# Full attention: who reads the turned row maxima out of PSUM, and who waits for whom over a score slot

## The reference

```python
scores = jnp.einsum('bhqd,bhkd->bhqk', q, k) / np.float32(np.sqrt(HD))
attn = jax.nn.softmax(scores, axis=-1)
out = jnp.einsum('bhqk,bhkd->bhqd', attn, v)
```

## Time and profile before

| | us |
|---|---|
| median of 3 runs | 4466.62 (4456.62 to 4467.39) |
| profiled execution, its own time | 4465.89 |
| its span, first to last instruction | 4464.1 |
| around the span | 1.79 |
| full attention, exponentials only | 279.2 to 1677.6 |
| first 31 groups' part of it | 278 to 1622 |

### The profile page before, as it was taken

The page is one execution under the profiler, slowest core; times in us unless marked ns, Lnnn a source line. Parts: engine busy times, 40 slices in busy tenths (PEclk is TensorE's granted clock), DMA queues, the critical chain, the costliest instruction groups (busy, mean ns, idle before and its releaser), DMA issues. The chain is left out here.

```text
span 4464.1 us, 79549 instructions
## 1 busy us (share of the span) xinstructions
PE 4130.9 (93%) x26918; PEld 2629.4 (59%) x26918; DVE 3555.6 (80%) x7972; ACT 2784.3 (62%) x6236; POOL 1568.3 (35%) x2441
## 2 busy tenths in 40 slices
PE   6679999999999986499999998999899999998998
PEld 3323333333333324377777776888777777777887
DVE  6589999999999957788888886656688888885665
ACT  3438888888888871167766665444567666663343
POOL 0000001000000003456655554454456555554555
PEclk9979999999999987799999999999999999998999
DMA  6833343233332306510000100221010010101321
GB/s 223 283 55 55 50 77 57 41 57 46 52 53 44 57 7 210 163 44 26 25 26 27 39 24 19 86 60 55 20 48 25 25 28 25 39 17 57 88 72 56
DMA packets 366416, 274.97 MB, mean 62 GB/s; under 512 B 98921, under 2 KB 333241, under 8 KB 366017
## 3 DMA queue, kind: packets, MB, share of 16 engines
q1 hardware_dynamic: 364608, 269.02, 24.7%
q10 hardware_dynamic: 1408, 0.93, 0.1%
HBM read 165.98 MB, written 102.81 MB: 60 GB/s over the span
## 5 line engine op out<-in xcount | busy, mean ns | idle before, releaser
L881 ACT ACTIVATE fa_P<-fa_pS 128x512 f32<-128x512 f32 x2048 | 1111.7, 595 | 324.9 <-PE fa_pS L805 276.1
L908 DVE TENSOR_REDUCE fa_mx<-fa_pR 128x2 f32<-128x1024 f32 x1024 | 1205.3, 1220 | 92.0 <-PE fa_pR L786 77.6
L1668 POOL TENSOR_TENSOR wa_pn<-wa_pr,wa_ri 128x512 f32<-128x512 f32 (+1 forms) x512 | 673.1, 1316 | 495.4 <-DVE wa_ri L1720 495.1
L1606 ACT ACTIVATE wa_pr<-wa_sm,wa_mn 128x256 f32<-128x256 f32 (+1 forms) x1024 | 496.7, 488 | 177.8 <-DVE wa_mn L1711 151.5
L822 PE MATMUL fa_pO<-fa_P,fa_V 128*32 128x512 f32 x4096 | 555.6, 615 | 0.0
L805 PE MATMUL fa_pS<-fa_Q,fa_K 50*128 50x512 f32 x2048 | 512.0, 497 | 41.9 <-ACT fa_P L881 11.2
L805 PEld LDWEIGHTS fa_pS<-fa_Q,fa_K 50*128 50x128 f32 x2048 | 192.6, 185 | 526.5 <-ACT fa_P L881 439.7
L786 PE MATMUL fa_pR<-fa_K,fa_Q 48*128 48x512 f32 x2048 | 429.5, 463 | 55.2 <-DMA fa_K<-parts_d 36.2
L753 POOL COPY fa_V<-fa_Vc 128x512 f32<-128x512 f32 x32 | 19.6, 613 | 1243.8 <-DMA fa_Vc<-v_d 1243.8
L1457 PE MATMUL wa_pQK<-wa_wqkv,wa_xT 128*128 128x512 f32 x1536 | 423.6, 412 | 6.3 <-DVE wa_qa L1757 6.3
L1711 DVE CUSTOM_DVE_ANT_0 wa_sm<-wa_pS,wa_mask 128x256 f32<-128x256 f32 (+1 forms) x1024 | 356.9, 402 | 21.2 <-issue 16.4
(11 more groups left out here) (185 smaller groups left out, 7062.8 us busy)
## 6 DMA issues: line engine op xcount, KB each, us to landing
parts_d<-pj_parts SPq DMA_DIRECT2D x64, 512.0 KB, 4.1
fa_Q<-parts_d SPq DMA_DIRECT2D x192, 128.0 KB, 4.2
fa_K<-parts_d SPq DMA_DIRECT2D x192, 128.0 KB, 7.2
pj_x<-in_L_attn_x SPq DMA_DIRECT2D x16, 512.0 KB, 6.2
v_d<-pj_v SPq DMA_DIRECT2D x16, 512.0 KB, 6.0
fa_Vc<-v_d SPq DMA_DIRECT2D x32, 256.0 KB, 8.4
fa_Q<-fa_nrow SPq DMA_DIRECT2D x512, 2.0 KB
att_d<-fa_att SPq DMA_DIRECT2D x64, 128.0 KB, 2.2
```

The source lines that it names most:

```text
L881: nc.scalar.activation(Pr[:, k % 2, h, :], pS[:, (s * exped.per + u) % T, :], ACT.Exp).then_inc(exped.sem, 1)
L908: nc.vector.tensor_reduce(mx[:, q // QB, :, a, q % QB, kh], row_slot(), AX.X, ALU.max).then_inc(row_free, 1)
L1606: last = nc.scalar.activation(pr[:, hp % 2, hh, lo:], sm[:, hp % 2, hh, lo:], ACT.Exp, bias=mn[:, p, h:h + 1], scale=-1.0, accum_out=rs[:, ...
L1668: nc.gpsimd.tensor_tensor(pn[:, hp % 2, :, lo:], pr[:, hp % 2, :, lo:], inv, ALU.mult).then_inc(s["weighted"].sem, 1)
```

## The change

The two DVE instructions of `max_out` go. In their place ACT copies the 16 turned rows from the `pR` slot to a new SBUF tile `nraw` (`max_copy`), and POOL splits `nraw` into the high and the low part (`split`). In ACT's order the copy stands behind the first exponential of step 1 (half 1) and of step 9 (half 0 of the next group). The counter `row_free` no longer counts these uses: `freed` leaves them out, and PE's wait for a slot last held by turned maxima is for `max_copied`, which ACT's copy raises. SP's wait before the eight DMAs is for `max_split`, which POOL raises. In POOL's order `spread` is called one group ahead and stands between the two splits.

```diff
+        nraw = sb("fa_nraw", [MCOLS, 2, P])
...
+        max_uses = sorted(max_use(n, half) for n in range(GROUPS) for half in range(2))
+        def freed(use):
+            return use + 1 - sum(1 for m in max_uses if m <= use)
@@ SP
                 def max_rows(n, s, half):
-                    sp.wait_ge(row_free, max_use(n, half) + 1)
+                    sp.wait_ge(max_split.sem, max_split.upto(n, half + 1))
@@ POOL
+                def split(n, s, half):
+                    pool.wait_ge(max_copied.sem, max_copied.upto(n, half + 1))
+                    nc.gpsimd.tensor_copy(nrow[:, s, half, 0, :], nraw[:, half, :]).then_inc(highs.sem, 1)
+                    pool.wait_ge(highs.sem, highs.upto(n, half + 1))
+                    nc.gpsimd.tensor_tensor(nrow[:, s, half, 1, :], nraw[:, half, :],
+                                            nrow[:, s, half, 0, :].bitcast(F32),
+                                            ALU.subtract).then_inc(max_split.sem, 1)
                 def body(n, s):
-                    spread(n, s)
+                    split(n, s, 1)
+                    if not is_last(n):
+                        spread(n + 1, (s + 1) % NB)
                     if 0 <= n - PREPARE - 1 < wh.PIECES:
                         wh.high(pool, nc.gpsimd.tensor_copy, 0, n - PREPARE - 1)
                         wh.low(pool, 0, n - PREPARE - 1)
+                    if not is_last(n):
+                        split(n + 1, (s + 1) % NB, 0)
+                spread(0, 0)
+                split(0, 0, 0)
@@ PE, row_slot
-                    if not (isinstance(base, int) and base + k < ROW_T):
-                        pe.wait_ge(row_free, base + k - ROW_T + 1)
+                    last = base + k - ROW_T
+                    if last in max_uses:
+                        pe.wait_ge(max_copied.sem, max_uses.index(last) + 1)
+                    elif last >= 0:
+                        pe.wait_ge(row_free, freed(last))
@@ ACT
+                def max_copy(n, half):
+                    at = max_use(n, half)
+                    act.wait_ge(row_full, at + 1)
+                    if n >= 1:
+                        act.wait_ge(max_split.sem, max_split.upto(n - 1, half + 1))
+                    nc.scalar.copy(nraw[:, half, :], pR[0:MCOLS, at % ROW_T, 0, 0:P]).then_inc(max_copied.sem, 1)
...
                             nc.scalar.activation(Pr[:, k % 2, h, :], pS[:, (s * exped.per + u) % T, :],
                                                  ACT.Exp).then_inc(exped.sem, 1)
+                            if h == 0 and k == 1:
+                                max_copy(n, 1)
+                            if h == 0 and k == KB + 1 and not is_last(n):
+                                max_copy(n + 1, 0)
@@ DVE
-                def max_out(n, s, half):
-                    neg_row = row_slot()[0:MCOLS, 0, 0:P]
-                    nc.vector.tensor_copy(nrow[:, s, half, 0, :], neg_row).then_inc(highs, 1)
-                    dve.wait_ge(highs, 2 * n + half + 1)
-                    nc.vector.tensor_tensor(nrow[:, s, half, 1, :], neg_row, nrow[:, s, half, 0, :].bitcast(F32),
-                                            ALU.subtract).then_inc(row_free, 1)
...
-                            max_out(n, s, 1)
+                            use[1] += 1
...
-                            max_out(n + 1, (s + 1) % NB, 0)
+                            use[1] += 1
```

More of the change, by code:

```diff
@@ L646, in full_attention @@
         row_full, row_free = sem("row_full"), sem("row_free")
-        neg, highs = Signal(sem("neg"), 2), sem("highs")
+        neg, highs = Signal(sem("neg"), 2), Signal(sem("highs"), 2)
+        max_copied, max_split = Signal(sem("max_copied"), 2), Signal(sem("max_split"), 2)
         inverse = Signal(sem("inverse"), 2)
@@ L718, in store @@
                 def store(n, half):
-                    sp.wait_ge(row_free, sums_use(n, half) + 1)
+                    sp.wait_ge(row_free, freed(sums_use(n, half)))
                     b, g = n // NG, n % NG
@@ L886, in body @@
                             copy_out(n, 0)
+                max_copy(0, 0)
                 drive(act, body)
@@ L911, in negative @@
                 def negative(n, half):
-                    dve.wait_ge(row_free, use[0] + use[1])
+                    dve.wait_ge(row_free, freed(use[0] + use[1] - 1))
                     nc.vector.tensor_reduce(nm[:, half, :], mx[:, half].rearrange("p e a q k -> p (e a q) k"), AX.X,
                                             ALU.max, negate=True).then_inc(neg.sem, 1)
-                def max_out(n, s, half):
-                    neg_row = row_slot()[0:MCOLS, 0, 0:P]
-                    nc.vector.tensor_copy(nrow[:, s, half, 0, :], neg_row).then_inc(highs, 1)
-                    dve.wait_ge(highs, 2 * n + half + 1)
-                    nc.vector.tensor_tensor(nrow[:, s, half, 1, :], neg_row, nrow[:, s, half, 0, :].bitcast(F32),
-                                            ALU.subtract).then_inc(row_free, 1)
                 def divide(n, half):
@@ L938, in _ @@
                 negative(0, 0)
-                max_out(0, 0, 0)
+                use[1] += 1
                 for j in range(ROWS // 2, ROWS):
```

## The result

The changed kernel takes 4490.9 us (median of 14 runs, 4472.87 to 4494.74) against 4462.56 (14 runs, 4456.58 to 4470.61): a ratio of 1.0058, 95% interval 1.0047 to 1.0068. That is slower by 0.6%, or 21 to 30 us; 28.5 had been forecast.

What follows compares the result with a forecast made beforehand. The bound was taken to be a loop of latencies through PE and ACT. The profiled 4465.9 plus 28.5 (62 x 0.46) gave 4494.4, or 4495.1 us on the median; range 4486 to 4508.

Steps and rivals of the forecast that it cites:

- What bounds the stage: Ordinary step: a PE, ACT, PE loop of latencies sets its 2.60 us; neither DVE nor ACT is full.
- What the change takes from VectorE is worth nothing: DVE's 0.27 + 0.28 removed 62 times: idle time, worth at most 0.04 each on the loop, 2.5 us.
- ScalarE's copy returns the slot late, and the second scores wait in TensorE's order: Steps 1 and 9: copy ends 0.83 behind the first exponential, second scores at 1.22, sums 0.46 later (0.35 to 0.65).
- 62 of them, none given back: 62 of 64 copies delay the loop, with no outer clock to catch up with: 28.5 us, ends 22 and 40.
- ScalarE's other work, GpSimd, SP's queue, GpSimd's order: Later exponentials, POOL's split, SP's DMAs about 2.2 us later and `spread` behind the split: all covered, no cost.
- VectorE's relief: Rival: VectorE sets the pace, each of 62 steps gives back 0.55, time 4432 us; chance 0.02.
- The clock: Rival: new holes in PE's work lower its clock, 91 us more, 4586; chance 0.04 together with a late split.
- The hidden copy: Rival: the copy fits ACT's 0.34 idle in a step, time 4466 within 3; chance 0.05.

Runs made afterwards that it cites:

- one experiment: Kernel before with the sums in two column halves, the first ahead of the second scores, and the second row pair behind them: 4414.48 us, 0.9901.
- The spare copy: Kernel before plus a 16x128 ScalarE copy from SBUF into a tile nothing reads, in the change's places, nothing waiting for it: 4456.51 us, 0.9996.
- the split with VectorE's copy: Changed kernel with VectorE making the one copy out of PSUM in the old place, GpSimd splitting, ScalarE's copies taken out: 4450.66 us, 0.9994.
- the copy moved ahead: Changed kernel with ScalarE's copy ahead of the first exponential of the step: 4457.01 us, 1.0003 of the kernel before.
- the still later copy: Changed kernel with ScalarE's copy one exponential later, behind the second of the step: 4506.71 us, 1.0114 of the kernel before.
- the longer copy: Changed kernel with ScalarE copying all 512 columns of the slot's 16 partitions, GpSimd using the first 128: 4501.85 us, 1.0099 of the kernel before.

## Why the prediction was right

**What bounds the stage:** right. The loop of first scores, first exponential, second scores and sums was broken open in one experiment and the ordinary step fell from 2.60 to 2.48. VectorE at 93% did not bound it: 0.57 less work for it in a group gave 0.01. The prediction did not see how near TensorE's own queue is behind the loop.

**What the change takes from VectorE is worth nothing:** right, both in the change and with the copy left on VectorE. The saving of at most 2.5 us is not resolved: 0.01 in a group would be 0.3 us.

**ScalarE's copy returns the slot late, and the second scores wait in TensorE's order:** right, 62 times, each with the copy named as releaser. The size was 0.46 in a step and measured 0.395 over the groups, 0.37 of it in the step itself. The term that was mis-sized is the end of the copy: 0.83 was assumed, it is 0.73. The copy takes 0.24 and not 0.27, and starts 0.49 and not 0.56 behind the exponential's start. The 0.56 is a mean of three distances, of which the middle one, 0.69, is a wait for the second scores; the other two are 0.49 (rows in the last section). The earlier trace rows had it: two exponentials take 1.08, so the second starts 0.49 behind the first. With 0.49 and nothing else altered, the prediction's own sum gives 0.39 in a step and 24 us. The rest holds to 0.01: release 0.05, second scores 0.34 behind the row pair, the sums 0.33 behind those. The remaining 0.02 of the 0.395 is spread over the other steps of the group, under 0.01 in each; what causes it was not followed up.

**62 of them, none given back:** right in number; 62 x 0.395 = 24.5 us of a profiled difference of 25.8 and a measured one of 21 to 30. The median's difference, 28.3, agrees with the forecast's 28.5 better than the mechanism does; that is chance. The runs of either kernel spread over 14 to 22 us, and in the profiled ones most of such a spread is the clock of the last group.

**ScalarE's other work, GpSimd, SP's queue, GpSimd's order:** right, nothing. The spare copy, the split with VectorE's copy and the copy moved ahead show it one by one. The split took 0.28 and 0.45, under the bounds of 0.61 and 0.95.

**The rivals:** VectorE's relief is out. The Trainium skill's page Perfetto Trace Analysis, section Optimizing Scalar/DVE Operations, says that it may make sense to take work off a saturated VectorE. At 93% busy this gave 0.01 in a group here, and with ScalarE as the taker a loss, so the measurement decides against using the busy share as the test. The clock stayed at 1.00 from 300 to 1655 us of the changed kernel, and from 300 to 1720 with the still later copy, so the longer holes did not bring it down. The evidence for that rival was also weaker than it looked. The half clock of the earlier trace rows belongs to that execution: in the second profile of the same kernel the last group has the same holes, a clock of 1.00 and steps of 2.61, not 4.06. The hidden copy was not what happened, but it is what one gets when the copy stands ahead of the exponential.

## What to carry to other kernels

When the release of a buffer moves to another engine, what counts is the place of the releasing instruction in that engine's order, and what stands behind the waiting one in its own. The Trainium skill says on its page PSUM — Partial Sum Buffer, section Engine vs sequencer instructions, that ScalarE's queue is strictly first in, first out. The traces agree: the copy starts 0.49 behind the first exponential with one exponential ahead of it in the order, and 0.97 with two. The same copy cost 0.85, 0.40 or 0.02 us a time behind the second, behind the first and ahead of the first exponential. A busy share of 93 or 98% is no proof of a bound; find the instruction that starts the next step and ask what it waited for. If a stage is a loop of latencies through two engines, look for work of the waiting engine that fits into the hole: here half of the sums, worth 1% of the whole kernel. And where the profile merges instructions into one row, take their distances one by one before using the mean: one of them may hold a wait.

## What the runs showed of the hardware that was not expected

A ScalarE instruction whose input is ready starts about 0.1 before the end that the profile gives for the one ahead of it. The merged rows hide this. These are the four exponentials of the ordinary step of the earlier trace rows, kernel before, asked for one at a time (timeline):

```profile
813.80 0.60 ACT L881 ACTIVATE fa_P<-fa_pS 128x512 f32<-128x512 f32 x1 [0.34 <-PE fa_pS L805]
814.30 0.59 ACT L881 ACTIVATE fa_P<-fa_pS 128x512 f32<-128x512 f32 x1
814.98 0.60 ACT L881 ACTIVATE fa_P<-fa_pS 128x512 f32<-128x512 f32 x1
815.48 0.59 ACT L881 ACTIVATE fa_P<-fa_pS 128x512 f32<-128x512 f32 x1
```

The second and the fourth start 0.49 (0.50 by the rounded rows) behind the one ahead. Only the third, which needs the second scores, starts 0.69 behind. The 16x128 copy starts 0.49 behind its exponential too, takes 0.24, and the next exponential starts 0.15 behind it. For its 16x512 form the timeline of the longer copy has:

```profile
820.98 0.60 ACT L913 ACTIVATE fa_P<-fa_pS 128x512 f32<-128x512 f32 x1
821.47 0.56 ACT L898 COPY fa_nraw<-fa_pR 16x512 f32<-16x512 f32 x1
821.93 0.58 ACT L913 ACTIVATE fa_P<-fa_pS 128x512 f32<-128x512 f32 x1
```

So what each takes of the queue is its own length less 0.09 to 0.10: 0.49 for an exponential of 0.60, 0.15 for a copy of 0.24, 0.46 for a copy of 0.56. The release of a buffer comes at the end of the full length, as the row pair's load 0.05 behind the copy's end shows.

The copy's length goes with its columns and hardly with its partitions: 16x512 takes 0.56, 128x512 out of the sums' bank 0.59.
